# A third half-image buffer with paced DMAs, and the PSUM banks dealt out anew

## What is computed

```python
x = x + _L0_conv_ref(_gn(x), ...)   # 3x3 depthwise conv, its weights mixed per image, then 1x1
x = x + _L1_conv_ref(_gn(x), ...)   # below
# _L1_conv_ref, c2 = 64, patches of 8 x 8 pixels
hidden = einsum('oc,bchw->bohw', w_hidden, x)          # 32 -> 192 channels
hidden = conv3x3_depthwise(hidden, w_dw)
q, k, v = split(hidden, 3, axis=1)
out = irfft2(rfft2(to_patch(q)) * rfft2(to_patch(k)))  # per patch, per channel
out_norm = (out - mu) / sqrt(var + 1e-05) * norm_w + norm_b    # over the 64 channels of a pixel
return einsum('oc,bchw->bohw', w_out, v * out_norm)
```

## Time and profile before

| | |
|---|---|
| median of 3 runs | 2653.68 us (2650.85 to 2656.28) |
| the profiled execution | 2649.98 us, span 2648.2 us |
| busy in the span | PE 88%, PE weight loads 56%, DVE 61%, ACT 55%, POOL 18% |
| granted PE clock, mean | 0.945 of full speed |
| DMA | 248.63 MB, mean 94 GB/s |

### The profile page before, as it was taken

One profiled execution on the slowest core, in us unless ns is written; L12 is line 12 of the kernel. 1 busy time (PEld: TensorE's weight loads), 2 busy tenths in 40 slices (PEclk: granted clock), 3 DMA queues, 4 the chain that ended last, 5 costly groups with the idle time before them and its releaser, 6 DMA issues. The chain is left out here.

```text
span 2648.2 us, 107033 instructions
## 1 busy us (share of the span) xinstructions
PE 2332.2 (88%) x48375; PEld 1493.1 (56%) x48375; DVE 1610.3 (61%) x4058; ACT 1453.6 (55%) x2629; POOL 476.6 (18%) x324
## 2 busy tenths in 40 slices
PE   7898888698989889898998988989889899998997
PEld 3333333466656566565665666656666566665664
DVE  5667666466656566565665666656666556665565
ACT  3556555655555555555555555555555555555552
POOL 1000000022222222222222222222222222222222
PEclk9899889799999999999999999999999999999999
DMA  6788887723232232222322223222232222322222
GB/s 132 195 234 232 228 219 211 181 71 72 70 72 65 68 73 68 65 62 69 71 70 66 62 69 72 67 67 59 69 74 68 68 52 70 74 68 68 56 51 50
DMA packets 60409, 248.63 MB, mean 94 GB/s; under 512 B 12393, under 2 KB 12658, under 8 KB 53810
## 3 DMA queue, kind: packets, MB, share of 16 engines
q1 hardware_dynamic: 59954, 241.78, 38.0%
HBM read 140.02 MB, written 101.72 MB: 91 GB/s over the span
## 5 line engine op out<-in xcount | busy, mean ns | idle before, releaser
L451 POOL TENSOR_TENSOR arena<-arena 128x8 f32<-128x8 f32 x256 | 452.3, 1767 | 1666.1 <-DVE arena L1123 1661.1
L587 PE MATMUL bank<-arena 128*64 128x512 f16 x4608 | 689.8, 393 | 0.0
L815 ACT ACTIVATE arena<-bank 100x512 f32<-100x512 f32 x1024 | 605.2, 628 | 96.8 <-PE bank L568 75.6
L1201 DVE TENSOR_TENSOR arena<-bank,arena 128x512 f32<-128x512 f32 x512 | 334.7, 685 | 412.9 <-issue 322.8
L568 PEld LDWEIGHTS bank<-arena 128*36 128x36 f16 (+1 forms) x8192 | 330.9, 104 | 232.3 <-issue 25.1
L522 PE MATMUL bank<-arena 32*32 32x508 f32 (+1 forms) x9216 | 377.2, 637 | 50.1 <-issue 35.2
L568 PE MATMUL bank<-arena 128*36 128x128 f16 (+1 forms) x8192 | 389.9, 221 | 17.5 <-DVE arena L1107 9.6
L857 ACT ACTIVATE arena<-bank 128x512 f32<-128x512 f32 x256 | 153.2, 599 | 442.1 <-PE bank L648 440.1
L648 PE MATMUL bank<-arena 100*32 100x128 f32 x8192 | 311.2, 288 | 87.6 <-issue 85.9
L677 PE MATMUL bank<-arena 32*64 32x256 f32 x8192 | 303.0, 417 | 83.6 <-ACT arena L870 46.6
L662 PE MATMUL bank<-arena 100*32 100x128 f32 x8192 | 302.6, 285 | 36.7 <-issue 36.5
(11 more groups left out here) (112 smaller groups left out, 1615.6 us busy)
## 6 DMA issues: line engine op xcount, KB each, us to landing
arena<-xn_d SPq DMA_DIRECT2D x128, 536.2 KB, 8.4
xn_d<-arena SPq DMA_DIRECT2D x130, 260.0 KB, 4.8
x_d<-arena SPq DMA_DIRECT2D x64, 512.0 KB, 8.3
arena<-x_d SPq DMA_DIRECT2D x128, 256.0 KB, 5.0
out<-arena SPq DMA_DIRECT2D x128, 256.0 KB, 4.3
arena<-x_in SPq DMA_DIRECT2D x32, 544.0 KB, 9.8
arena<-x_in SPq DMA_DIRECT2D x32, 528.0 KB, 9.6
arena<-spectra_in SPq DMA_DIRECT2D x1, 384.0 KB
```

The costliest lines, as they stand in the source:

```text
L451: pool.tensor_tensor(tiny["rstd"][:, slot], tiny["var_eps"][:, slot], powers, ALU.pow).then_inc(s_root, 1)
L587: mm = pe.matmul(v_banks[chunk % 3][64 * s:64 * s + 64, :], v_w[:, 64 * tap:64 * tap + 64], at(xs[half], row * WP + 32 * k + dx, [32 * WP, ...
L815: act.activation(h_rows[0:WIN, :, first:first + 4], ring[g % len(ring)][0:WIN, :].rearrange("p (i c) -> p c i", i=4), ACT.Copy).then_inc(s ...
L1201: dve.tensor_tensor(prod[:, first:first + 512].rearrange("p (a b x) -> p a b x", a=2, b=2), at(k_banks[m % 2], 256 * quad, [128, 2], [0, 2 ...
```

## The change

A third half-image buffer `xs_late` is taken from memory that stage 1 has left, and unit u uses `xs[u % 3]`. SP loads the half image of u + 1 once the first hidden group of u is done, and waits for each of the four DMAs before it issues the next (`paced`). The four stores of a result are paced in the same way. The residual comes in two halves of two DMAs, the first after the third inverse batch of its unit, the second when the first has landed. One of the four window buffers goes, for room: windows 0 to 2 of the next unit are cut in the spectral step, window 3 in the front. The PSUM banks get new owners, so that batch e = 3 goes to banks 0, 1, 2 and 6 (those of q, k, the ring and the projection), and e = 0 to 2 stay in 3, 5, 7 and 4. The waits on PE follow the owners. The first two half images, in stage 1, are loaded unpaced as before.

The core of the diff (functions are named where their head is left out; the rest passes u in place of b and half):

```diff
-        ring_banks = [banks[1], banks[3], banks[7]]
-        v_banks = [banks[2], banks[5], banks[0]]
-        q_bank = banks[0]
-        k_banks = [banks[1], banks[2]]
-        i_banks = [banks[3], banks[5], banks[7], banks[4]]
+        t_bank, f_bank = banks[4], banks[6]
+        ring_banks = banks[0:3]
+        q_bank, k_banks = banks[0], banks[1:3]
+        v_banks = [banks[3], banks[5], banks[7]]
+        inverse_banks, last_inverse_banks = v_banks + [t_bank], ring_banks + [f_bank]
+        def i_banks(e):
+            return inverse_banks if e < 3 else last_inverse_banks
...
-        xs = [take(HALF * WP, f16) for _ in range(2)]
+        xs = [take(HALF * WP, f16) for _ in range(2)] + [xs_late]
-        win = [take(1632, f16) for _ in range(4)]
+        win = [take(1632, f16) for _ in range(3)]
...
-            def load_xs(b, half):
+            def load_xs(u, paced=True):
+                b, half = divmod(u, 2)
                 for g in range(4):
-                    sp.dma_start(xs[half][32 * g:32 * g + 32, :], src).then_inc(s_xs_in[half], 16)
+                    sp.dma_start(xs[u % 3][32 * g:32 * g + 32, :], src).then_inc(s_xs_in[u % 3], 16)
+                    if paced:
+                        sp.wait_ge(s_xs_in[u % 3], 64 * (u // 3) + 16 * (g + 1))
...
+            def load_res(u, pair):
+                for s in range(2):
+                    p0 = 64 * pair + 32 * s
+                    sp.dma_start(res[p0:p0 + 32, :].rearrange("p (l r) -> p l r", l=2),
+                                 image_rows(x2_d, u // 2, u % 2, pair, s)).then_inc(s_res_in, 16)
+            def store_res(u):
+                y = out.rearrange("b c h w -> b c (h w)")
+                sp.wait_ge(s_res_done, 4 * (u + 1))
+                for part in range(4):
+                    pair, s = divmod(part, 2)
+                    sp.dma_start(image_rows(y, u // 2, u % 2, pair, s),
+                                 res[32 * part:32 * part + 32, :].rearrange("p (l r) -> p l r", l=2)).then_inc(s_out_stored, 16)
+                    sp.wait_ge(s_out_stored, 64 * u + 16 * (part + 1))
...
-            def unit_dma(u, prev, here, nxt):
-                sp.wait_ge(s_v_mm, 8 * u)
-                if nxt is not None:
-                    load_xs(*nxt)
-                sp.wait_ge(s_res_done, 4 * u)
-                store_res(*prev)
-                sp.wait_ge(s_out_stored, 64 * u)
-                if here is not None:
-                    load_res(*here)
+            for u in range(1, LAST + 1):
+                if u < LAST:
+                    sp.wait_ge(s_hidden_mm, 32 * u + 1)
+                    load_xs(u + 1)
+                store_res(u - 1)
+                sp.wait_ge(s_inverse_mm, 4 * u + 3)
+                load_res(u, 0)
+                sp.wait_ge(s_res_in, 64 * u + 32)
+                load_res(u, 1)
+            store_res(LAST)
...
             def hidden_group(u, g, ring):
-                if g in (1, 2) and positive(16 * u):
-                    pe.wait_ge(s_y_ready, 16 * u - (3, 1)[g - 1])
+                if g < 3 and positive(16 * u):
+                    pe.wait_ge(s_y_ready, 16 * u - 3 + g)
-                w = win[g // 4 % 4]
+                w = win[(8 * u + g // 4) % 3]
...
+            def v_chunk(u, k, jr, groups, between):
                 chunk = 2 * k + jr
-                if chunk == 0:
-                    pe.wait_ge(s_prod_ready, 16 * (u + 1))
-                if chunk == 1:
-                    pe.wait_ge(s_y_ready, 16 * (u + 1) - 2)
-                if chunk == 2:
-                    pe.wait_ge(s_q_copied, 8 * (u + 1))
-                if chunk > 2:
+                if chunk < 3:
+                    pe.wait_ge(s_y_ready, 16 * u + 9 + chunk)
+                else:
                     pe.wait_ge(s_gated, 8 * u + chunk - 2)
...
                 def k_octet(m):
                     if positive(16 * u + 2 * m - 2):
                         pe.wait_ge(s_prod_ready, 16 * u + 2 * m - 2)
-                    if m == 1 and tail is not None:
-                        pe.wait_ge(s_gated, 8 * u - 1)
...
                 def inverse(e):
                     pe.wait_ge(s_prod_ready, 16 * u + 4 * e + 4)
-                    if positive(16 * u + 4 * e):
+                    if 0 < e < 3:
                         pe.wait_ge(s_y_ready, 16 * u + 4 * e)
+                    if e == 3 and tail is not None:
+                        pe.wait_ge(s_res_done, 4 * u)
-                                mm = pe.matmul(i_banks[c][64 * lam:64 * lam + 64, 256 * (e % 2):256 * (e % 2) + 256],
+                                mm = pe.matmul(i_banks(e)[c][64 * lam:64 * lam + 64, 256 * (e % 2):256 * (e % 2) + 256],
...
+            def window(u, r):
-                if positive(32 * u + 4 * (r - 3)):
-                    dve.wait_ge(s_hidden_mm, 32 * u + 4 * (r - 3))
+                if positive(32 * u + 4 * (r - 2)):
+                    dve.wait_ge(s_hidden_mm, 32 * u + 4 * (r - 2))
...
+            def front(u, tail):
-                rows = iter(range(4, 8) if u is not None else ())
+                rows = iter(range(3, 8) if u is not None else ())
...
                     if p == 1:
                         centre(tail, 0)
+                windows()
                 scale(tail, 0)
...
+            def spectral(u, tail):
...
-                    if nxt is not None and n in (8, 10, 11, 13):
-                        window(nxt[0], nxt[1], (8, 10, 11, 13).index(n), nxt[2])
+                    if u < LAST and n in (8, 10, 12):
+                        window(u + 1, n // 2 - 4)
```

More of the change, by code:

```diff
@@ L111, in build @@
         s_transforms_in = semaphore("transforms_in")
-        s_xs_in = [semaphore(f"xs_in{s}") for s in range(2)]
+        s_xs_in = [semaphore(f"xs_in{s}") for s in range(3)]
         s_res_in = semaphore("res_in")
@@ L240, in build @@
         v_w = take(9 * 64, f16)
-        dw_t = take(128)
         powers = take(8)
@@ L261, in build @@
         ones_row = take(128)
+        dw_t = take(128)
         st1, st2 = take(6 * NCH), take(6 * NCH)
@@ L280, in build @@
         res = take(2048)
+        xs_late = take(HALF * WP, f16)
         top[0] = max(top[0], stage1_end)
-        xs = [take(HALF * WP, f16) for _ in range(2)]
+        xs = [take(HALF * WP, f16) for _ in range(2)] + [xs_late]
         G_q = take(64 * 64)
         G_k = take(64 * 64)
-        win = [take(1632, f16) for _ in range(4)]
+        win = [take(1632, f16) for _ in range(3)]
         block = ctx.enter_context(nc.Block())
@@ L362, in _ @@
                 if b == NB + 1:
-                    load_xs(0, 1)
+                    load_xs(1, paced=False)
                 if older is not None:
@@ L428, in _ @@
             pool.memset(xl.bitcast(f32), 0.0).then_inc(s_pads_zero, 1)
-            for s in range(4):
+            for s in range(3):
                 pool.memset(win[s][:, 16 * WIN:1632].bitcast(f32), 0.0).then_inc(s_win_room, 1)
@@ L587, in v_chunk @@
                         mm = pe.matmul(v_banks[chunk % 3][64 * s:64 * s + 64, :], v_w[:, 64 * tap:64 * tap + 64],
-                                       at(xs[half], row * WP + 32 * k + dx, [32 * WP, 2], [WP, 8], [1, 32]),
+                                       at(xs[u % 3], row * WP + 32 * k + dx, [32 * WP, 2], [WP, 8], [1, 32]),
                                        start=tap == 0, stop=tap == 8)
@@ L610, in project @@
                 mm.then_inc(s_project_mm, 1)
-            def front(u, half, tail):
+            def front(u, tail):
                 groups = iter(range(32 if u is not None else 0))
@@ L626, in front @@
                     return
-                v_half = 1 - half
                 hidden(3)
                 for k in range(4):
-                    v_chunk(tail, v_half, k, 1, (5, 5, 4, 3)[k], hidden)
+                    v_chunk(tail, k, 1, (5, 5, 4, 3)[k], hidden)
                     if k > 0:
@@ L634, in front @@
                     if k < 3:
-                        v_chunk(tail, v_half, k + 1, 0, (5, 4, 3)[k], hidden)
+                        v_chunk(tail, k + 1, 0, (5, 4, 3)[k], hidden)
                     if k < 3 or u is None:
                         turn(tail, k, 1)
-            def spectral(u, half, tail):
+            def spectral(u, tail):
                 def q_octet(m):
@@ L696, in spectral @@
                 inverse(3)
-                v_chunk(u, half, 0, 0, 0, None)
-            front(0, 0, None)
-            spectral(0, 0, None)
-            for b in range(NB - 1):
-                for half in (1, 0):
-                    u = 2 * b + 2 - half
-                    front(u, half, u - 1)
-                    spectral(u, half, u - 1)
-            front(LAST, 1, LAST - 1)
-            spectral(LAST, 1, LAST - 1)
-            front(None, 0, LAST)
+                v_chunk(u, 0, 0, 0, None)
+            front(0, None)
+            spectral(0, None)
+            for u in range(1, LAST + 1):
+                front(u, u - 1)
+                spectral(u, u - 1)
+            front(None, LAST)
```

(34 more changed lines are left out.)

23 lines of the change are left out of this document (8 added, 15 removed).

## The result

| | before | changed |
|---|---|---|
| median | 2653.16 us (2650.85 to 2656.28, 4 runs) | 2360.10 us (2354.59 to 2366.28, 4 runs) |
| ratio of the runs | | 0.8895 (95% interval 0.887 to 0.8921) |
| profiled execution | 2649.98 us | 2366.28 us |
| granted PE clock, mean | 0.945 | 0.972 |

A forecast was written before the change was run, and what follows sets the result against it. PE was taken as the bound, held by late program blocks and bank waits. Savings of 288.6 + 5.0 + 1.4 less 7.5 = 287.5 us gave 2362.5 us profiled, 2366 us median; range 2345 to 2400 us, chance 0.63.

The forecast's parts named there:

- Two costs bound PE's pace, banks and late program blocks: PE, units 1 to 30: 153.7 us stand as issue waits and 43.7 us for ACT's copies out of shared banks.
- The "issue" waits are PE's program behind SP's sets: PE in mid-matmul: program blocks of some 254 instructions come late behind SP's DMA sets, 153.7 us in 60 pieces.
- 56.0 us for a unit without stalls: A full unit after the change: unit 31's clean 51.77 us plus the matmuls missing from it, 56.0 us.
- 0.35 us for window 3: Front: DVE's window 3 copy ahead of the scale makes PE's first transposes wait 0.35 us, bounds 0 and 0.6.
- 0.3 us for paced stores: Spectral part, end of the tail: four single store DMAs still cost PE 0.3 us a unit in stalls and clock.
- Unit 31, 5.0 us: Last unit, 61.68 us from batch to batch before the change: it saves 5.0 us.
- 7.5 us at the end: End of the span: the last four stores in series take 14.0 us instead of 6.5, so 7.5 more.
- SP's chain of 45.6 us: SP: load quarters, residual halves and store quarters, all waiting in one chain, take 45.6 us and fit a 56 us unit.
- The slower rival: SP's chain becomes the bound: 72 us a unit, DVE waits for the half image, the kernel takes 2834 us; chance 0.03.
- The sum: Whole kernel: units 1 to 30 save 288.6 us, unit 31 5.0, unit 0 1.4, less 7.5 at the end: 287.5.
- 2362.5 us for the profiled execution, 3.7 more for the median: Whole kernel: 2649.98 us less 287.5 gives 2362.5; the median of the runs is 3.7 higher, so 2366 us.
- one full stall a unit, from the store or from a residual half: Rival, at the store or the batch's end: 2.25 + 1.8 = 4.1 us a unit, 2489 us; chance 0.14.

## Why the prediction was right

- *Two costs bound PE's pace, banks and late program blocks.* Right, and shown to be separate: new banks alone leave 147.4 of 153.7 us of issue waits. The bank term was 1.47 us a unit; the bank wait gave that (43.7 us in 30 units), and the whole edit alone 2.14.
- *The "issue" waits are PE's program behind SP's sets.* Right: with fewer bytes in the same DMAs they fall from 153.7 to 57.6 us, and in the spectral step at once they return, one a unit, each ended by a packet of PE's program. One reading was loose: two queues are named "instruction", and the stretch of the earlier trace rows holds one packet of 0.01 MB of the other, q14. It has 74 packets in the whole kernel, too few for PE's program, so the argument stands. That a block comes behind the whole set was too strong: in the pair of store and residual, blocks come late from inside the sets.
- *56.0 us for a unit without stalls.* Measured 56.13 in the kernel with window 3 later, which has neither the scale's wait nor more than 0.8 us of issue waits in 30 units.
- *0.35 us for window 3.* 9.0 us in 30 pieces, 0.30, by the waits; 0.38 by the kernel with the copy one place later (56.51 to 56.13).
- *0.3 us for paced stores.* Over-sized: all issue waits of 30 units together are 0.9 us, 0.03 a unit. The unit was forecast at 56.65 and took 56.51, so about half of this error was covered by the 0.1 that the base was short.
- *Unit 31, 5.0 us.* Measured 61.68 to 56.64, 5.04.
- *7.5 us at the end.* Measured 4.4 (40.8 to 45.2). A store quarter takes 2.8 us (the last store's first three in 8.3), not 3.5; the row I took it from had the load's traffic ahead.
- *SP's chain of 45.6 us.* In unit 15: the load about 21 us (1307.21 to 1328), the store 11.7 (8.96 to the last issue, 2.7 to land), the residual's halves some 10 (5.92 to the last issue, 4.2 to land), 43 in all, and SP waits for DVE before the store. The slower rival had nothing to stand on.
- *The sum.* 30 x (66.23 - 56.51) + 5.0 - 4.4 = 292, against 283.7 in the two profiled executions. The missing 8 are ahead of unit 1: the last batch of unit 0 comes at 558.9 us in the profile before and at 567.2 in the changed one. Nothing ties them to the change: over the 13 profiled executions it falls anywhere from 556.7 to 569.2, and in the kernel with small loads, whose program up to there is that of the kernel before, it comes at 566.6. What makes it move stays open, and the 1.4 us forecast for unit 0 can't be read beside it.
- *2362.5 us for the profiled execution, 3.7 more for the median.* The profiled execution took 2366.3. The 3.7 came from the runs of the kernel before and had the wrong sign here: the profiled execution was the slowest of the changed kernel's, and the median is 6.2 us under it. That the forecast of 2366 meets the profiled 2366.28 is luck; against the median it was 6 us too high.

Two steps had the mechanism in part wrong, without harm to the sum. I wrote that each quarter of the load waits for the one before and that this keeps a block within 2.7 us; the load in one piece in the front does as well, so the place (and the third buffer that permits it) earns what I put to place and pacing together. And I priced "one full stall a unit, from the store or from a residual half" by unit 31 as if the residual's set alone had made that stall. It takes the unbroken pair of store and residual; the residual alone, right behind a paced store, costs 0.5 us by the profiled execution and 0.7 by the medians, not 4.1.

In order of the cuts, as ratios of the kernel before: banks 2.6 points, the load into the front (with the third buffer and one window fewer) 4.7, the paced store 3.0, the late residual 0.7. The last two change places freely, since either does most of the work of both.

## What to carry to other kernels

When PE stands in the middle of a run of matmuls with no semaphore to name, look at what the DMA queues did in the 10 us before it: the program of a fully unrolled kernel arrives by the same engines as the data. Put large sets of DMAs beside the part in which PE takes longest for an instruction, and break up those that must stand beside short matmuls; it doesn't matter much which of two neighbouring sets is broken. What a pause costs includes the clock behind it, where it falls (1.8 us behind the 2.25 of unit 31).

## What the runs showed of the hardware

PE's program comes by the 16 DMA engines that serve the kernel, and the kernel's own DMAs make it late. Between the packet that ended a wait and the one before it lay 13.9 us (the middle one of the 31 waits with the load in the spectral step at once) and 6.4 us (with store and residual at once, 24 waits of over 0.7 us), where PE takes 3.5 us for a block. A set of four loads, 11 us of traffic, cost 6.3 us a unit there; store and residual, sets of 4.8 and 6.5 us with 1.3 us between them in unit 17, cost 3.5; each of the two alone cost 0.3 to 0.7. In the front, where PE takes 9.0 us for a block, the set of four loads cost 0.2.

The Trainium skill (DMA: Bandwidth & Descriptors, on queues and rings) has the engines take turns between queues at the border of a packet of descriptors. The trace agrees in that a block can come while a set is at work (at 1575.7, with the residual's packets running to 1578.2). How many descriptors go ahead of it no run here shows.

With the load paced in the spectral step PE paused up to 1.7 us at a time, 19.0 us in all, and the granted clock over 1700 us was 1.00. Behind the pause of 2.22 us in unit 17 of the variant with store and residual at once it was 0.58 over 7.7 us, the 1.2 GHz level for most of it. The length of the pause alone doesn't decide: in the same execution one of 2.63 us, which ended at 1760.16, left the clock at 1.00 over the next 6 us. What else decides was not looked at.
